# A four-layer kernel on one core: the packed weights fetched in two transfers, and the setup work of layers 1 to 3 issued among layer 0 of the first item

## The reference, cut to what matters

```
xn = layernorm(x)
x  = x + attn_i(xn, weights of i) * silu(ffn_i(xn, weights of i))     # i = 0, 1, 2, 3
```

## Time and profile before

| | |
|---|---|
| runs | 5222.0, 5226.68, 5237.3 us (median 5226.68) |
| the profiled execution's own time | 5220.98 us |
| its span, first to last instruction | 5219.2 us |
| mean granted TensorE clock | 0.822 of 2.4 GHz |
| PE busy | 3965.6 us (76%) |
| DVE busy | 3970.4 us (76%) |
| ACT busy | 2966.9 us (57%) |
| POOL busy | 2533.0 us (49%) |
| DMA, mean over the span | 8 GB/s |

### The profile page before, as it was taken

The page is one execution under the profiler, slowest core; times in us unless marked ns, Lnnn a source line. Parts: engine busy times, 40 slices in busy tenths (PEclk is TensorE's granted clock), DMA queues, the critical chain, the costliest instruction groups (busy, mean ns, idle before and its releaser), DMA issues. The chain is left out here.

```text
span 5219.2 us, 58396 instructions
## 1 busy us (share of the span) xinstructions
PE 3965.6 (76%) x16712; PEld 1848.2 (35%) x16712; DVE 3970.4 (76%) x7862; ACT 2966.9 (57%) x5742; POOL 2533.0 (49%) x2332
## 2 busy tenths in 40 slices
PE   5777788868878678777788677886887777877676
PEld 2332244423443234432344224442344323443233
DVE  3335678967889678886888868896788967888698
ACT  3443556645666456655666466664566645665443
POOL 1214255453555445562555625545455545556365
PEclk9876889968998789977899688996899878997555
DMA  1000000000000000000000000000000000000000
GB/s 81 1 25 0 5 1 1 25 3 3 1 25 1 3 3 1 25 1 3 3 1 25 1 5 1 8 18 3 3 1 25 1 3 3 1 25 1 2 1 3
DMA packets 7995, 44.07 MB, mean 8 GB/s; under 512 B 848, under 2 KB 848, under 8 KB 7248
## 3 DMA queue, kind: packets, MB, share of 16 engines
q1 hardware_dynamic: 7632, 39.89, 2.0%
HBM read 37.52 MB, written 2.36 MB: 8 GB/s over the span
## 5 line engine op out<-in xcount | busy, mean ns | idle before, releaser
L2054 DVE MAX8 m<-top 128x8 f32<-128x512 f32 x2048 | 1290.7, 679 | 6.4 <-ACT top L1988 5.9
L2117 POOL TENSOR_SCALAR top<-top,m 128x512 f32<-128x512 f32 x512 | 809.9, 1582 | 836.6 <-DVE m L2054 670.2
L2058 DVE MATCH_REPLACE8 top<-m,top 128x512 f32<-128x512 f32 x1536 | 1026.3, 675 | 0.2
L290 PE MATMUL bank<-arena,consts 128*128 128x512 f32 (+1 forms) x912 | 627.7, 782 | 90.7 <-POOL arena L1662 45.4
L2123 POOL TENSOR_TENSOR top<-top 128x512 f32<-128x512 f32 x512 | 654.6, 1278 | 37.5 <-ACT top L1996 20.2
L290 PE MATMUL bank<-arena,weights 128*128 128x512 f32 (+5 forms) x992 | 553.9, 678 | 65.8 <-DVE arena L1242 29.0
L1927 PE MATMUL bank<-consts,top 128*128 128x128 f32 x2048 | 389.5, 322 | 210.6 <-POOL top L2123 128.7
L290 PE MATMUL bank<-arena 128*64 128x128 f32 (+3 forms) x3200 | 464.3, 366 | 54.4 <-ACT arena L1105 53.8
L2003 ACT ACTIVATE top<-bank 128x512 f32<-128x512 f32 x512 | 305.5, 597 | 296.4 <-PE bank L1927 294.8
L1927 PEld LDWEIGHTS bank<-consts,top 128*128 128x128 f32 x2048 | 283.2, 165 | 489.8 <-POOL top L2123 274.8
L290 PE MATMUL bank<-top,vt 128*9 128x128 f32 x4096 | 340.7, 321 | 151.8 <-ACT top L2003 128.2
(11 more groups left out here) (297 smaller groups left out, 6436.9 us busy)
## 6 DMA issues: line engine op xcount, KB each, us to landing
arena<-experts_dram SPq DMA_DIRECT2D x32, 768.0 KB, 6.6
weights<-weights_dram SPq DMA_DIRECT2D x1, 6982.0 KB, 19.2
hold<-x_dram SPq DMA_DIRECT2D x9, 256.0 KB, 2.8
out_dram<-x_out SPq DMA_DIRECT2D x9, 256.0 KB, 3.5
consts<-consts_dram SPq DMA_DIRECT2D x1, 1759.5 KB, 23.6
rot<-consts_dram SPq DMA_DIRECT2D x1, 1024.0 KB, 25.6
```

What stands on the lines that cost most here:

```text
L290: return nc.tensor.matmul(o, lhsT, rhs, start=start, stop=stop)
L2054: nc.vector.max(m8[:, slot(p, e), k], src).then_inc(SB["top"], 1)
L2058: nc.vector.match_replace(wk_[e], m8[:, slot(p, e), k], sc[slot(p, e)] if k == 0 else wk_[e], -3e38).then_inc(SB["rest"], 1)
L2117: nc.gpsimd.tensor_scalar(pp[e], sc[slot(p, e)], m8[:, slot(p, e), TOPK // 8, 0:1], None, ALU.is_ge).then_inc(SB["kept"], 1)
```

## The change

The weights are packed with layer 0's first (and the coupling weights of layer 3), up to `cut`, the first column that belongs to layer 1: 1938 of 13964 columns, 969 KB. SP now issues five transfers: the weights up to `cut`, x0 and the constants, which raise `loaded` (48 in all), and behind them the other weights and `rot`, which raise a semaphore of their own, `rest` (32). The setup block keeps ACT's three copies and DVE's fills and 8 small multiplications, and its PE stream is gone. All else of the setup becomes three generators, `late_pe`, `late_act` and `late_dve`, which `also` draws, one step behind each step of layer 0 from the thirteenth on (step 12, which is n = 3 of the loop), in the first run only. `late_pe` and `late_act` are one step each, `late_dve` is five. PE's results go to `X[0]` and `X[1]` in place of `A[0]` and `A[1]`, the head sums to `top` in place of `arena`. After `late_act` the kernel no longer knows ACT's table, so the next step loads one.

```diff
+        late_marks = Marks(nc, ctx, "late")
+        SL = late_marks.layer(DMA="rest 2", PE="by_channel 1,shifts 1", ACT="exp_a 1,alpha 1",
+                              DVE="head_sum 2,head_mean 1,by_channel_sb 1")
+        head_sum = top[:, 0:4 * H3].rearrange("p (n g) -> p n g", n=2)
...
-                    sp.dma_start(w_sb[:], w_in).then_inc(S["loaded"], 16)
+                    sp.dma_start(w_sb[:, 0:cut], w_in[:, 0:cut]).then_inc(S["loaded"], 16)
                     sp.dma_start(x0, x_in[0]).then_inc(S["loaded"], 16)
                     sp.dma_start(c_sb[:], c_in[:, 0:once]).then_inc(S["loaded"], 16)
-                    sp.dma_start(rot[:].rearrange("p n t -> p (n t)"), c_in[:, once:]).then_inc(S["loaded"], 16)
+                    sp.dma_start(w_sb[:, cut:], w_in[:, cut:]).then_inc(SL["rest"], 16)
+                    sp.dma_start(rot[:].rearrange("p n t -> p (n t)"), c_in[:, once:]).then_inc(SL["rest"], 16)
...
+        def late_pe(pe):
+            S = SL
+            pe.wait_ge(S.sem["rest"], 32)
+            for n, (name, part) in enumerate((name, part) for name in ("gamma", "beta") for part in range(2)):
+                r = nc.tensor.transpose(X[0][:, 128 * n:128 * n + 128], W(f"l3_{name}", lo=128 * part, n=128), C("ident"))
+            r.then_inc(S["by_channel"], 1)
...                                       (the 18 one-column products, as before, into X[1])
+            r.then_inc(S["shifts"], 1)
+            yield
+        def late_act(a):
+            S = SL
+            a.wait_ge(S.sem["rest"], 32)
+            act(a_neg[:], W("l2_alog"), ACT.Exp).then_inc(S["exp_a"], 1)
+            act(alpha[:, 0], W("l3_alpha"), ACT.Sigmoid).then_inc(S["alpha"], 1)
+            now[0] = None
+            yield
+        def late_dve(v):
+            S = SL
+            v.wait_ge(S.sem["rest"], 32)
+            v.wait_ge(*S("exp_a", 1))
...                                       (a_neg, alpha, head sums and means: step 1)
+            yield
+            v.wait_ge(*S("shifts", 1))
...                                       (mix_bias and 6 adds: step 2; 4 gains and 6 adds: step 3; 4 gains: step 4)
+            yield
+            v.wait_ge(*S("by_channel", 1))
...                                       (by_channel and keep: step 5)
+        def also(steps, more):
+            for n, kind in enumerate(steps):
+                if n >= 12:
+                    next(more, None)
+                yield kind
+            for _ in more:
+                pass
...
-            yield from l0_pe(pe)
+            yield from also(l0_pe(pe), late_pe(pe)) if first else l0_pe(pe)
```

More of the change, by code:

```diff
@@ L320, in clear @@
             nc.all_engine_barrier()
+        late_marks = Marks(nc, ctx, "late")
+        SL = late_marks.layer(DMA="rest 2", PE="by_channel 1,shifts 1", ACT="exp_a 1,alpha 1",
+                              DVE="head_sum 2,head_mean 1,by_channel_sb 1")
+        head_sum = top[:, 0:4 * H3].rearrange("p (n g) -> p n g", n=2)
         with ExitStack() as c0:
             marks = Marks(nc, c0, "setup")
-            S = marks.layer(DMA="loaded 4", PE="by_channel 1,shifts 1", ACT="exp_a 1,alpha 1",
-                            DVE="head_sum 2,head_mean 1,by_channel_sb 1")
-            head_sum = arena[:, 0:4 * H3].rearrange("p (n g) -> p n g", n=2)
+            S = marks.layer(DMA="loaded 3")
+            cut = wcols["l1_ln_w0"][0]
             with nc.Block(no_gpsimd_drain=True) as block:
@@ L331, in _ @@
                 def _(sp):
-                    sp.dma_start(w_sb[:], w_in).then_inc(S["loaded"], 16)
+                    sp.dma_start(w_sb[:, 0:cut], w_in[:, 0:cut]).then_inc(S["loaded"], 16)
                     sp.dma_start(x0, x_in[0]).then_inc(S["loaded"], 16)
                     sp.dma_start(c_sb[:], c_in[:, 0:once]).then_inc(S["loaded"], 16)
-                    sp.dma_start(rot[:].rearrange("p n t -> p (n t)"), c_in[:, once:]).then_inc(S["loaded"], 16)
[L337 to L350, removed]
+                    sp.dma_start(w_sb[:, cut:], w_in[:, cut:]).then_inc(SL["rest"], 16)
+                    sp.dma_start(rot[:].rearrange("p n t -> p (n t)"), c_in[:, once:]).then_inc(SL["rest"], 16)
                 @block.scalar
                 def _(a):
-                    a.wait_ge(S.sem["loaded"], 64)
+                    a.wait_ge(S.sem["loaded"], 48)
                     act(pick[:], C("pick"), ACT.Copy)
@@ L357, in _ @@
                     act(eye[:], C("ident"), ACT.Copy)
-                    act(a_neg[:], W("l2_alog"), ACT.Exp).then_inc(S["exp_a"], 1)
-                    act(alpha[:, 0], W("l3_alpha"), ACT.Sigmoid).then_inc(S["alpha"], 1)
                 @block.vector
@@ L365, in _ @@
                     nc.vector.memset(vt[:, :, :, D3:D3 + 1], 1.0)
-                    v.wait_ge(S.sem["loaded"], 64)
+                    v.wait_ge(S.sem["loaded"], 48)
                     for n, lay in enumerate(("L0", "L3")):
@@ L372, in _ @@
                         ts(couple[:, n, 3:4], W(f"{lay}_gc_b3"), 0.5, None, ALU.mult)
[L373 to L400, removed]
             clear(marks.sems.values())
@@ L2163, in b_pool @@
             yield from l3_pool(g, cp)
-        def a_pe(pe):
-            yield from l0_pe(pe)
+        def late_pe(pe):
[4 more added lines that the diff above has]
+            r.then_inc(S["by_channel"], 1)
+            for i in range(DEPTH):
+                for n, name in enumerate(("Wk", "Wv", "Wr")):
+                    mm(X[1][:, DEPTH * n + i:DEPTH * n + i + 1], W(f"l1_{name}{i}"), W(f"l1_ln_b{i}"))
+                for n, (o, w) in enumerate(HCH):
+                    at = 8 + 6 * i + 2 * n
+                    mm(X[1][0:w, at:at + 1], W(f"l1_w1_{i}", lo=o, n=w), W(f"l1_lb{i}"))
+                    r = mm(X[1][0:w, at + 1:at + 2], W(f"l1_w1_{i}", lo=HID + o, n=w), W(f"l1_lb{i}"))
+            r.then_inc(S["shifts"], 1)
+            yield
@@ new lines, in late_act @@
+        def late_act(a):
[9 more added lines that the diff above has]
+            v.wait_ge(*S("exp_a", 1))
+            ts(a_neg[:], a_neg[:], -1.0, None, ALU.mult)
+            v.wait_ge(*S("alpha", 1))
+            ts(alpha[:, 1], alpha[:, 0], -1.0, 1.0, ALU.mult, ALU.add)
+            heads = [W(name, n=256).rearrange("p (g d) -> p g d", d=D3) for name in ("l3_qkv", "l3_bqkv")]
+            for n, w3 in enumerate(heads):
+                nc.vector.tensor_reduce(head_sum[:, n], w3, AX.X, ALU.add).then_inc(S["head_sum"], 1)
+            v.wait_ge(*S("head_sum", 2))
+            ts(head_sum, head_sum, 1.0 / D3, None, ALU.mult).then_inc(S["head_mean"], 1)
+            v.wait_ge(*S("head_mean", 1))
+            for n, w3 in enumerate(heads):
+                tt(w3, w3, head_sum[:, n, :, None].to_broadcast([128, 2 * H3, D3]), ALU.subtract)
+            yield
+            v.wait_ge(*S("shifts", 1))
+            for n, share in enumerate((0.5 * (1.0 - 0.95), 1.0, 0.5)):
+                ts(mix_bias[:, n], X[1][:, DEPTH * n:DEPTH * n + DEPTH], share, None, ALU.mult)
+            for i in range(DEPTH):
+                for n, (o, w) in enumerate(HCH):
+                    for part, name in enumerate(("b1a", "b1g")):
+                        at, b = 8 + 6 * i + 2 * n + part, W(f"l1_{name}{n}_{i}")
+                        tt(b, b, X[1][0:w, at:at + 1], ALU.add)
+                yield
+                for name, gain in (("Wk", "ln_w"), ("Wv", "ln_w"), ("Wr", "ln_w"), ("w1_", "lg")):
+                    ts(W(f"l1_{name}{i}"), W(f"l1_{name}{i}"), W(f"l1_{gain}{i}"), None, ALU.mult)
+            yield
+            v.wait_ge(*S("by_channel", 1))
+            nc.vector.tensor_copy(by_channel[:], X[0][:, 0:512:128]).then_inc(S["by_channel_sb"], 1)
+            v.wait_ge(*S("by_channel_sb", 1))
+            for n, kept in enumerate(("quarter", "group32", "quarter", "group32")):
+                ts(keep[:, n], C(kept), by_channel[:, n:n + 1], None, ALU.mult)
+            yield
@@ L2169, in a_pe, with a_act @@
+        def also(steps, more):
[5 more added lines that the diff above has]
+                pass
+        def a_pe(pe, first):
+            yield from also(l0_pe(pe), late_pe(pe)) if first else l0_pe(pe)
             yield from l1_pe(pe)
             yield from l2_pe(pe)
-        def a_act(a):
-            yield from l0_act(a)
+        def a_act(a, first):
+            yield from also(l0_act(a), late_act(a)) if first else l0_act(a)
@@ L2177, in a_dve @@
         def a_dve(v, first):
-            yield from l0_dve(v, first)
+            yield from also(l0_dve(v, first), late_dve(v)) if first else l0_dve(v, first)
             yield from l1_dve(v)
@@ L2206, in _ @@
                 def _(pe):
-                    weave(a_pe(pe) if item else None, b_pe(pe) if search else None)
+                    weave(a_pe(pe, first) if item else None, b_pe(pe) if search else None)
                 @block.scalar
                 def _(a):
-                    weave(a_act(a) if item else None, b_act(a) if search else None)
```

(4 more changed lines are left out.)

## The result

The changed kernel took 5179.28 us (median of four runs, 5175.79 to 5183.58), beside 5224.93 us for the kernel before (5222.0 to 5237.3). The ratio is 0.9909, 95% interval 0.9891 to 0.9926. It is 46 us faster; 18.4 were forecast, with 5195 as the lower end of the range. The profiled execution took 5175.79 us, its span is 5173.8.

A forecast was written before the change was run, and what follows sets the result against it. Transfers bound the start, PE bounds layer 0. Terms -17.0 - 11.35 + 6.4 + 2.5 + 0.85 + 0.2 = -18.4 us, put on the median of 5226.68 us, gave 5208 us; range 5195 to 5220.

The forecast's parts named there:

- Transfers: Setup's wait for data: awaited transfers end at 10.8 us instead of 27.77, saving 17.0 us.
- Tail: Setup work after the transfers: 1.52 us left of 12.87, saving 11.35 us before layer 0's first product.
- Clock at the start: Layer 0's opening: removing the setup's products takes no warm clock away, 0 us, bound +-3 us.
- Inserted work: Setup work moved beside layer 0 of the first item: 9.95 us put in.
- PE's part: Late transposes and one-column products in layer 0, all on the path: 6.4 us (4.6 to 8.2).
- a slow stretch behind it: Layer 0 after the late narrow products: granted clock falls to half, costing 2.5 us (0 to 4).
- the reload: ACT loads the coupling's table again before round 2's Gelu in layer 0: 0.85 us on the path.
- The bound on ACT's and DVE's parts: Late work in layer 0: if PE's work did not cover ACT's, at most 1.5 us more would show.
- rival B: Cheap insertion into layer 0: PE's work 4.6 us, no further slow stretch; -23 us, 5204 us; chance 0.09.
- what is gained or lost here moves the end one for one: First item: nothing runs beside it and blocks end in barriers, so its savings pass fully to the total.
- the prediction's own signs: Wrong if layer 0 grows by more than 14 or less than 5 us, or later time changes beyond scatter.
- a shifted clock pattern in the remaining 5100 us: Time after the start: a changed clock pattern might make the kernel slower; within the 0.04 chance for slower.

The follow-up runs named there:

- e3: Changed kernel with the late steps left out and constants in place of their results: 5140.37 us.
- e1: Kernel before with its weights split into two transfers, all five transfers still awaited in the setup: 5225.31 us, ratio 1.0006.
- e5: Kernel before with eight more, never used semaphores cleared at the first run's end: 5183.90 us, ratio 0.9924.
- e7: Kernel before with a separate block of 3 DVE fills between the first run and the loop: 5213.83 us, ratio 0.998.
- e9: Kernel before with eight of its own semaphores cleared a second time at the first run's end: 5171.20 us, ratio 0.991.
- e14: Kernel before with four of its own semaphores cleared a second time at the first run's end: 5204.44 us, ratio 0.9957.
- e6: Changed kernel with the late steps' eight semaphores cleared after the last run instead of the first: 5202.74 us, ratio 0.9952.
- e13: Changed kernel, late steps' semaphores cleared after the last run, eight others cleared again at the first run's end: 5180.39 us, ratio 0.9918.
- e4: Changed kernel with 28 DVE fills of 512 columns added in the setup block: 5191.75 us.

## Why the prediction was wrong, step by step

- **Transfers.** Landing 10.8 us forecast, 10.39 measured; saved 17.4 for 17.0. Right, also that what is queued behind costs the first three nothing, and that `rest` is long met (it landed at 24.6 and 27.1 us; first asked for near 42).
- **Tail.** First product at 12.3 forecast, 11.75 measured: 28.89 us earlier for 28.35. Right. No fetch or slowing beside the transfers showed: ACT's first 128x512 instruction beside them took 0.60 us.
- **Clock at the start.** Counted as 0. Layer 0's first product takes 2.05 us in both; the four products behind them (eight instructions, from 47.61 and 18.72) take 5.15 us before and 5.51 after. So without the setup's products the opening is 0.36 us longer: small, as forecast.
- **Inserted work.** Forecast 9.95 us. The traces give +4.16 (before to after), 6.9 (e3 to after), and 5.9 as the difference of means: layer 0 took 80.64, 82.46, 77.86, 82.17, 78.32 and 77.93 us in the six kernels of the old form (before, e1, e5, e7, e9, e14), 79.9 on average, and 84.00 to 88.05 in the nine that have the late steps from step 12 on, 85.8 on average. Oversized were three terms. PE's part took 4.2 us, not 6.4: I set the middle between two clock levels, and the late work met the upper one. Then 2.5 us for a slow stretch behind it: the clock did fall (46.56), but of layer 0's own slow stretches one is not there any more (25 to 35 us behind the first product the clock is 0.70 and 0.62 before, 1.00 and 0.95 after). And the reload: PE's idle time before the Gelu's product grew by 0.27 us, not 0.85. (The bound on ACT's and DVE's parts, 4.3 + 2.0 less 4.6, is 1.7 us and not the 1.5 written there.) So the direct part lies closer to rival B, the cheap insertion with -23 us, than to the forecast. The drain that the Trainium skill ("ScalarE: Activation LUTs", What ACT_TABLE_LOAD costs) puts behind a table load is again not there: the second load, of 1.28 us, is followed by its ACTIVATE at 45.22 with nothing between.
- **The failed step: "what is gained or lost here moves the end one for one".** The sum stopped at the first run's end, and called the clearing of eight semaphores "a cost below 0.1 us", for which no row stood. It cost 0.24 us in the first run and gave some 20 us or more back in the loop: 5202.7 us without these clears, 5179.3 and 5180.4 with them; in the kernel before 5217 to 5227 (medians of five sets of runs) without, 5171 and 5184 with. The direct part, -22.9 us measured in e6, agrees with the -18.4 of the sum within its interval (the sum's own range, 5202 to 5214 us, just holds e6's 5202.7); in the two profiled executions the first run ends 24.5 us earlier. That the forecast direction came true is owed to this part; that the end is 46 us away is not foreseen anywhere. By the prediction's own signs it was wrong twice: layer 0 grew by 4.16 us in the profiled pair (5 was the least), and the time after the first run changed by 20.8. The rivals had no such case; the one place that spoke of it, a shifted clock pattern in the remaining 5100 us, had 0.04 with slower only.
- **How it works, as far as the runs show.** The kernels' rounds are alike up to where the granted clock rises or falls a little earlier or later, and then differ by steps of some us; round 1 of before, e1 and e6 has a stretch of 30 us at 0.50 to 0.52 that the fifteen kernels with a longer gap do not have. The later rounds follow in ever other patterns between 605 and 625 us, or settle (four rounds of 617.8 us in before and in e6). That the clears at the first run's end remove that stretch and shorten the kernel is shown by e5, e6, e9 and e13, with e14 half-way. That they do it through the gap, and not through the place of the loop's code, which they also move by an instruction or two on each engine, is argued and not tested alone. For the gap speak e4, whose loop code lies 28 instructions further back on DVE and whose round 1 is the changed kernel's to 0.02 us, and the DMA queues that fetch instructions: in the first 136 us of the loop they carry the same 2 and 3 packets in before, e6, e9 and the changed kernel. Not shown are the rule by which the clock answers to the gap, and why loops at one gap differ: 4270 to 4274 us in e3, e5 and e9, 4296 to 4302 in the changed form. Something beside the gap has a part in it. As executions of one kernel differ too (5211 to 5250 us for the kernel before in one set), the length of a single profiled loop is no more than one draw.

## What to carry to other kernels

When a loop's body has a matmul engine whose clock rises and falls, its length is one of several, and an edit ahead of it can change which: put a chance of both signs on it, here some 20 to 45 us of 5200. Before crediting a gain to an edit, split the span at marks that both traces have (a store per item) and look for a difference in stretches that the edit doesn't touch; then try the edit's by-products alone. And a control with a few idle clears shows how wide such a kernel's "no change" is.

## What the runs showed of the hardware that was not expected

- Eight semaphore clears spread over five engines lengthen the meeting at a block's end by 0.24 us, four by 0.12 (gaps 5.64, 5.76, 5.87 us), sixteen by 0.36 (6.00) and twenty-four by 0.59 (6.23).
- The clock's pattern in the first 230 us of round 1 is the same for loops that start at 498, 505, 521 and 525 us with the same gap ahead: there it goes with the program's own course and not with a time of its own.
- The 36 one-column instructions with their weight loads take 7.12 us in the old setup and 3.93 in layer 0 (granted clock 0.95 in 42.70 to 46.70 us). The first is the lower clock by the product that follows, 2.05 us for two instructions, though the granted clock prints 1.00 there.
